# A decoder layer's scan stage: the scores move to two pairs of PSUM banks and lead each slot on TensorE, and the decays' two-place ring moves from PSUM to SBUF

## What is computed

```
x = x + attention(layernorm(x))                # causal, 16 heads of 32, 2 key/value heads, then Wo and bo
x = x + ssm(ctx, z=layernorm(x))               # selective state space model, 512 channels, 16 states
x = x + experts(layernorm(x))                  # 16 experts of which 2 per token, and a shared one
```

```
state[t] = state[t-1] * exp(dt[t] * A[n]) + (dt[t] * u[t]) * B[t, n]
y[t]    += state[t] * C[t, n]
```

## Time and profile before

| | |
|---|---|
| Median of 3 runs | 1161.83 us (1160.21 to 1162.95) |
| Profiled execution, its own time | 1163.83 us |
| Its span, first to last instruction | 1162.1 us |
| Mean granted TensorE clock | 0.984 of full |
| Busy: PE, DVE, ACT, POOL | 1067.5, 826.7, 666.0, 678.5 us |

### The profile page before, as it was taken

The page is one execution under the profiler, slowest core; times in us unless marked ns, Lnnn a source line. Parts: engine busy times, 40 slices in busy tenths (PEclk is TensorE's granted clock), DMA queues, the critical chain, the costliest instruction groups (busy, mean ns, idle before and its releaser), DMA issues. The chain is left out here.

```text
span 1162.1 us, 19085 instructions
## 1 busy us (share of the span) xinstructions
PE 1067.5 (92%) x6650; PEld 651.8 (56%) x6650; DVE 826.7 (71%) x1244; ACT 666.0 (57%) x1442; POOL 678.5 (58%) x587
## 2 busy tenths in 40 slices
PE   7999978888888888888888999999999989999994
PEld 3454545656556556656665544444444467777761
DVE  6988689999999999999999486640680134434428
ACT  3767789999999999999999324202011012333320
POOL 3022299999999999999999450202043035555530
PEclk9999979999999999999999999999999989999997
DMA  7310111101111111112231043102225424444229
GB/s 217 93 38 13 27 28 38 37 28 38 37 38 28 38 38 33 33 38 80 85 110 47 1 146 109 73 37 72 73 78 199 166 75 135 135 131 132 75 74 387
DMA packets 51966, 94.75 MB, mean 82 GB/s; under 512 B 9950, under 2 KB 18142, under 8 KB 51872
## 3 DMA queue, kind: packets, MB, share of 16 engines
q1 hardware_dynamic: 44352, 72.82, 19.5%
q0 software_dynamic: 7520, 20.72, 5.7%
HBM read 74.51 MB, written 20.84 MB: 82 GB/s over the span
## 5 line engine op out<-in xcount | busy, mean ns | idle before, releaser
L699 POOL TENSOR_TENSOR w_all<-w_all 128x512 f32<-128x512 f32 x256 | 320.5, 1275 | 16.2 <-POOLq L96 16.2
L925 DVE TENSOR_TENSOR_SCAN w_all<-da,w_all 128x512 f32<-128x512 f32 x256 | 298.1, 1205 | 1.1 <-POOL w_all L699 0.9
L857 ACT ACTIVATE da<-w_all,a_flat 128x512 f32<-128x512 f32 x256 | 180.3, 705 | 2.3 <-DVE w_all L925 1.6
L793 PE MATMUL yb<-ident,w_all 128*128 128x128 f32 x1024 | 160.4, 280 | 20.9 <-DVE acc L933 20.7
L865 ACT ACTIVATE w_all<-sc,neg_max 128x128 f32<-128x128 f32 (+3 forms) x256 | 134.3, 541 | 15.7 <-DVE neg_max L917 14.7
L793 PEld LDWEIGHTS yb<-ident,w_all 128*128 128x128 f32 x1024 | 115.6, 142 | 45.6 <-issue 23.9
L743 PE MATMUL sc<-w_all,attn 32*128 32x384 f32 (+3 forms) x512 | 105.6, 489 | 27.2 <-ACT w_all L865 21.9
L1352 POOL TENSOR_TENSOR w_all<-w_all 128x512 f32<-128x512 f32 x24 | 29.4, 1226 | 156.1 <-ACT w_all L1548 156.1
L874 ACT ACTIVATE w_all<-tb 128x256 f32<-128x256 f32 (+2 forms) x192 | 103.0, 536 | 27.8 <-PE tb L758 27.7
L917 DVE TENSOR_REDUCE neg_max<-sc 128x2 f32<-128x256 f32 (+3 forms) x128 | 104.1, 813 | 19.9 <-PE sc L746 15.8
L1874 DVE COPY attn<-w_all 128x512 f32 x94 | 40.3, 429 | 108.2 <-PE pe L1815 106.7
(11 more groups left out here) (222 smaller groups left out, 1651.4 us busy)
## 6 DMA issues: line engine op xcount, KB each, us to landing
w_all<-b_scratch SPq DMA_DIRECT2D x64, 256.0 KB, 3.3
w_all<-in_w_up SPq DMA_DIRECT2D x16, 512.0 KB, 5.5
w_all<-in_w_down SPq DMA_DIRECT2D x16, 512.0 KB, 6.7
w_all<-sorted_y SPq DMA_DIRECT2D x16, 512.0 KB, 10.0
attn<-in_x SPq DMA_DIRECT2D x4, 1024.0 KB, 6.9
w_all<-in_x SPq DMA_DIRECT2D x16, 256.0 KB, 4.3
norms<-attn SPq DMA_DIRECT2D x4, 1024.0 KB, 4.3
out_dram<-acc SPq DMA_DIRECT2D x16, 256.0 KB, 9.3
```

The lines of the kernel that those rows point to most:

```text
L699: pool.tensor_tensor(dbu[:, k, :], keep["du"][i // N][:, k * T:(k + 1) * T], b_all[i % 2][:, :], ALU.mult).then_inc(pool_dbu.sem, pool_dbu ...
L793: last = pe.transpose(yb[which][:, k * P:(k + 1) * P], state[i % 2][:, k, t * P:(t + 1) * P], ident[:, :])
L857: act.activation(da[unit % 2][:, :], keep["dt"][i // N][:, k * T:(k + 1) * T], ACT.Exp, scale=keep["a_flat"][:, unit % (N * KD):unit % (N ...
L925: dve.tensor_tensor_scan(state[i % 2][:, k, :], da[unit % 2][:, :], dbu[:, k, :], 0.0, ALU.mult, ALU.add).then_inc(dve_scan.sem, dve_scan. ...
```

## The change

`sc` becomes two tensors of two banks, chosen by unit mod 2. `da` keeps two places but lies in SBUF, since the eight banks are full. `scores(g + 1)` stands first in slot g on PE, and waits for the exponents of unit g - 1. `out_bank` uses the four score banks; its first waits are changed accordingly.

```
-        sc = ctx.enter_context(nc.psum_tensor("sc", [P, 2, 512], F32))
-        da = [pb(f"da{i}") for i in range(2)]
+        sc = [ctx.enter_context(nc.psum_tensor(f"sc{i}", [P, 2, 512], F32)) for i in range(2)]
+        da = [sb(f"da{i}", [P, T]) for i in range(2)]
...
-        out_bank = [sc[:, 0, :], sc[:, 1, :], da[0][:, :], da[1][:, :]]
+        out_bank = [sc[n // 2][:, n % 2, :] for n in range(4)]
...
-                if 2 * unit >= 1:
-                    pe.wait_ge(act_p.sem, act_p.upto(2 * unit - 1))
+                if unit >= 2:
+                    pe.wait_ge(act_p.sem, act_p.upto(2 * (unit - 2) + 1))
...
-                    pe.matmul(sc[:, x, 0:n], keep["attn"][r:r + DH, b, m * T + j * P:m * T + (j + 1) * P],
+                    pe.matmul(sc[unit % 2][:, x, 0:n], keep["attn"][r:r + DH, b, m * T + j * P:m * T + (j + 1) * P],
...
                     if n == 0:
                         pe.wait_ge(keep["s_wo"].sem, keep["s_wo"].upto(KD - 1))
+                        pe.wait_ge(act_p.sem, act_p.upto(2 * UNITS - 3))
+                    if n == 2 * KD:
                         pe.wait_ge(act_p.sem, act_p.upto(2 * UNITS - 1))
-                    if n == 2 * KD:
-                        pe.wait_ge(dve_scan.sem, dve_scan.upto(2 * UNITS - 1))
...
             for g in range(UNITS):
                 late = (g - 3) % NT >= 2
+                if g + 1 < UNITS:
+                    scores(g + 1)
                 if 0 <= g - 2 < UNITS and late:
                     turn_state(g - 2, 0)
...
-                if g + 1 < UNITS:
-                    scores(g + 1)
                 if g >= 2 and spread_in(g) is not None:
```

More of the change, by code:

```diff
@@ L738, in scores @@
                     pe.wait_ge(s_k.sem, s_k.upto(KEYS - 1))
-                if 2 * unit >= 1:
-                    pe.wait_ge(act_p.sem, act_p.upto(2 * unit - 1))
+                if unit >= 2:
+                    pe.wait_ge(act_p.sem, act_p.upto(2 * (unit - 2) + 1))
                 for x in range(2):
                     r = (2 * half + x) * DH
-                    pe.matmul(sc[:, x, 0:n], keep["attn"][r:r + DH, b, m * T + j * P:m * T + (j + 1) * P],
+                    pe.matmul(sc[unit % 2][:, x, 0:n], keep["attn"][r:r + DH, b, m * T + j * P:m * T + (j + 1) * P],
                               k_4[r:r + DH, b, m // 2, 0:n], start=True, stop=False)
                 for x in range(2):
-                    last = pe.matmul(sc[:, x, n - P:n], ident_bf[:, :], mask[:, :], start=False, stop=True)
+                    last = pe.matmul(sc[unit % 2][:, x, n - P:n], ident_bf[:, :], mask[:, :], start=False, stop=True)
                 last.then_inc(pe_s.sem, pe_s.tick(unit))
@@ L864, in exponent @@
                     act.wait_ge(dve_max.sem, dve_max.upto(unit))
-                act.activation(prob[:, x, off[j]:off[j] + n], sc[:, x, 0:n], ACT.Exp, bias=neg_max[unit % 2][:, x:x + 1],
+                act.activation(prob[:, x, off[j]:off[j] + n], sc[unit % 2][:, x, 0:n], ACT.Exp, bias=neg_max[unit % 2][:, x:x + 1],
                                           accum_out=row_sum[unit // 8 % 2][:, 2 * half + x, j:j + 1]).then_inc(act_p.sem, act_p.tick(2 * unit + x))
@@ L916, in top @@
                 dve.wait_ge(pe_s.sem, pe_s.upto(unit))
-                dve.tensor_reduce(neg_max[unit % 2][:, :], sc[:, :, 0:n], AX.X, ALU.max, negate=True).then_inc(dve_max.sem, dve_max.tick(unit))
+                dve.tensor_reduce(neg_max[unit % 2][:, :], sc[unit % 2][:, :, 0:n], AX.X, ALU.max, negate=True).then_inc(dve_max.sem, dve_max.tick(unit))
             def scan(unit):
```

## The result

The changed kernel takes 1369.81 us (median; 1369.45 to 1372.58) against 1161.93: 1.180 times as long, 95% interval 1.178 to 1.182. The forecast was 1388 with a range of 1360 to 1455: the direction and the mechanism hold, the size is 18 us too large.

A forecast was written before the change was run, and what follows sets the result against it. The prediction took DVE and POOL, each 96% busy in the scan stage, as the bound; the profiled 1163.83 us + 225.6 (collision) - 1.1 (out-projection) gave 1388.3, put at 1388, range 1360 to 1455.

The forecast's parts named there:

- Part 1: Scan stage: decays' ring moves from PSUM to SBUF, so scans and POOL operations take turns; slot of 5.68 us, +225.6 us.
- With one SBUF input nothing of it is seen: DVE operations with one SBUF input do not collide with POOL; the scan stage's maximum and accumulation add no turns.
- The sum: Scan-stage slot: turns add to 5.51 us, 5.60 or 5.76 with pitches by order; middle 5.68 taken, +225.6 us.
- Rival A: Scan stage: the scan does not collide and DVE loses its 14.7 us of waits for scores; 1146 us; chance 0.05.
- Rival B: Scan stage: row after row, no overlap at the handover; slot 6.23 us, kernel 1459 us; chance 0.10.
- Rival C: Scan stage: PE's clock falls, and PE is the bound if it stays low; slot 6.28, kernel 1465 us; chance 0.10.
- below 1.00 over the stage: Sign to look for: a granted PE clock under 1.00 over the scan stage would mean Rival C is the case.
- Part 2: Scan stage: scores get two bank pairs and lead PE's slot; DVE's 14.7 us of waits go, worth nothing at 5.68 us slots.
- Part 3: Out-projection: starts earlier, in the other pair of banks; PE's 1.1 us wait in front of it goes, -1.1 us.

The follow-up runs named there:

- e1: The kernel before with the decays' ring in SBUF as the only change; 1369.32 us, 1.179 times the kernel before.
- e2: The kernel before with one of the two places of the decays' ring in SBUF, the other in PSUM; 1254.14 us, 1.079.
- e3: The changed kernel with POOL's three operations per slot replaced by memsets, so POOL writes but does not read; output not right; 1152.01 us, 0.992.
- e4: The kernel before with POOL's three operations per slot replaced by memsets; output not right; 1160.33 us, 0.999.
- e8: The kernel before with DVE running the first scan ahead of the maximum in slots with the widest scores; 1175.84 us, 1.012.
- e5: The changed kernel with POOL's two products per slot replaced by scalings that read one SBUF tensor; 1246.71 us, 1.072.

## Why the prediction was right, and where its size was off

Part 1, the collision: shown by e1 (the ring's place alone is the whole loss), e2 (only the scans with two SBUF inputs pay) and e3 (it needs POOL's reading). The reading of one DVE and one POOL operation in another stage of the trace, where each row was longer than its kind by the rest of the other, carried over to the scan. One sentence beside it is too wide: "With one SBUF input nothing of it is seen". In its own the normalisation of L1613, which reads one SBUF tensor and two columns, takes 1.49 us beside POOL's bias adds, and 0.54 for the later batches. This didn't reach the sum, since the maximum and the accumulation of the scan stage did keep their lengths.

The sum put the slot at 5.68; it is 5.545, and 127 x 0.135 = 17 us is the error. Two terms were mis-sized. The first is the order. I took the middle between scan, POOL, scan, POOL, POOL (5.60) and scan, scan, POOL, POOL, POOL (5.76), the latter from the earlier trace rows, where DVE operations with overlapping rows kept POOL out for 4.72 us: besides the five of L568 shown there, one before them and the scaling of L564 at 21.01. Scans do not: a POOL operation got in behind each of the 256, so only the first order occurs. That is 0.08. The second is what each one needs behind the other: 1.067 for POOL (predicted 1.13) and 1.081 for the scan (1.06), together 0.075 less in a slot; 0.02 came on top as gaps between the turns. The scans' rows overlap too (305.58 against an end at 305.65), so overlap isn't what keeps POOL out. Why the convolution's operations do and scans do not is open: no run took it apart.

Rival A (no collision) is refuted by the rows. Its 14.7 us of gain isn't confirmed either: where almost nothing collides the change gives 8 us (e3 against e4), and most of DVE's wait turns up at `normalize`. Rival B (row after row, 6.23): the ends lie 1.067 and 1.081 apart, not a full row of 1.274 or 1.206. The Trainium skill's rule ("SBUF — State Buffer", "SBUF: two separate sides") is right about this pair, reading included; its "whole instruction", taken as the row's length, is 0.2 us too long for the POOL operation here and 0.12 for the scan. Rival C (PE's clock): it did fall, to 0.85 over the stage, and cost nothing that can be seen: PE stands 115.4 us for DVE's accumulation, and e1 has the same stage at 0.81. So the prediction's sign for it, "below 1.00 over the stage", was no sign: it appeared without C's price.

Part 2: DVE's waits for scores went as forecast, worth nothing here (e1).

Part 3 matches by luck. The rest of the kernel is 1.28 us shorter, with 1.1 forecast, but not where the forecast had it. Cut at the first instruction of L1600, where the experts stage begins on DVE (kernel before, then the changed one):

```profile
644.41:668.13 23.72, 21.60 (x137) 11.83 (x135) 8.10 (x13) 6.50 (x13) 8.93 (x10) 1.00 0.00 1
668.13:1162.10 493.97, 472.31 (x1946) 275.03 (x1946) 229.75 (x493) 105.36 (x175) 159.29 (x152) 0.98 0.36 123
851.59:875.73 24.14, 22.75 (x139) 13.10 (x138) 9.59 (x13) 6.50 (x13) 12.37 (x11) 0.96 0.00 1
875.73:1368.00 492.27, 471.09 (x1946) 273.97 (x1946) 229.59 (x493) 105.36 (x175) 159.16 (x152) 0.98 0.37 124
```

The stretch with the out-projection is 0.4 us longer, though PE's wait in front of it is gone. What became shorter is the experts stage, which no edit touches; over the eight profiles of kernels with the right output it takes 491.6 to 495.1 us. The first scan 1.25 us sooner is no sure effect either: in e8, whose code up to it is that of the kernel before, it also comes early, at 147.71.

## What to carry to other kernels

Before a tensor moves from PSUM to SBUF, count the SBUF inputs of every VectorE operation that reads it: here the scan with the second one takes turns with GpSimd's reads, and as both engines are near full that costs the sum of both instead of the larger. One SBUF input isn't always free either: see L1613 in the earlier trace rows. Look in the trace for rows of either engine that are longer than others of their form; they tell the price before anything is built. Then make two sums, one of what the engines take in turn and one of what each has to do by itself with its waits in it: in e5 the second was the larger, and was the slot. It needs the wait as it is: with a full 1.07 behind both scans the changed kernel's DVE would come to 5.76 us, above its 5.545, since a scan that follows other work of DVE finds POOL's operation already under way. And look at whom an edit delays before it removes a wait: of three that aim at the same 14.7 us, one gained 0.5% and two lost 1.2% and 3.2%.

## What the runs showed of the hardware that I had not expected

- GpSimd got in behind every one of the 256 scans, also when the next scan was ready, while it was kept out for 4.72 us by the convolution's multiply-adds and one scaling.
- VectorE's normalisation with one SBUF tensor (L1613) also takes turns with GpSimd's adds: 1.49 us beside them, 0.54 in the later batches. The statistics of L1600, which read one SBUF tensor as well, take 0.68 beside the same adds. No run took the difference apart.
- A GpSimd operation of 128x512 with two inputs needs 1.07 us behind a scan's end for a row of 1.27 alone, one with a single input 0.49 for 0.69 (after, e5).
